# Attention with fp16-split operands: the row-maximum scores as two full-height matmuls instead of two half-height ones, and the maximum's rows moved behind the head's

## The chip, the cores and the metric

The kernel runs on one core of one Trainium2 chip. Its time is the device time of one execution in microseconds (us); the kernel before was timed three times. PE is TensorE (PEld its weight loads), DVE VectorE, ACT ScalarE, POOL GpSimd, SP the engine whose queue issues the DMAs. L532 is line 532 of the kernel before.

## What is computed

One pre-norm transformer block in float32 over x of 4 x 1024 x 128: layer norm, attention with 16 heads of 64, a residual, a second layer norm, and a gated feed-forward part (width 352) whose inputs and weights are quantised in blocks of 16. The attention, which holds nearly all of the work:

```python
q, k, v = (split_heads(ln(x) @ W.T) for W in (Wq, Wk, Wv))     # 4, 16, 1024, 64
sim  = einsum('bhid,bhjd->bhij', q, k) * 64 ** -0.5
e    = exp(sim - max(sim, axis=-1))
attn = e / (sum(e, axis=-1) + 1e-10)
x    = x + (attn @ v).reshape(4, 1024, 1024) @ Wo.T + bo
```

## The kernel before

**Work.** A pair of heads of one batch element is a round; there are 32, and `rounds` runs 34, since a round overlaps three pairs: the next pair's projections, this pair's scores and exponentials, and the previous pair's output (`flags` says which parts a round has). A round has four units `k` (head `k // 2`, half `k % 2` of its 1024 queries), and a unit eight slots `s`. Every engine has its own program in this order, written out by hand. The table `JOBS` says at which unit and slot PE, ACT and DVE do a round's other jobs (projections `k0` to `v1`, the transpose `m` of the maxima, `t`/`o` for the output projection, `x g u h d` for the feed-forward part); on PE all of them stand at odd slots. Those of the feed-forward part run in two-round cycles from round 9 on.

**Number format.** q and k are each split into a high and a low fp16 part. Per head there are four 1024-column operands: `q_hl` has q high in partitions 0 to 63 and q low in 64 to 127; `k_hh` has k high twice; `q_hm` and `k_l1` hold, in 64 partitions each, q high and k low, and beside them two rows with the (negative) row maxima and two rows of a constant, so that the product of the two adds k low times q high and subtracts each query's maximum. The other 62 partitions of the second pair are zeroed once (`ones`, L716 to L720).

**A slot on PE.** The transposed scores of 128 keys against 512 queries, in PSUM `st`: a matmul of 128 rows and 512 columns of `k_hh` and `q_hl` (L548), then one of `k_l1` and `q_hm` (L550). ACT takes the exponential (L658), POOL computes its fp16 low part (L415). Then eight matmuls of 129 columns for the unit before, which accumulate probabilities times v in `ob` (L576).

**The row maxima.** The maximum must be known before the exponentials, so two units ahead PE also computes the scores the other way round, 128 queries against 1024 keys, in the two PSUM banks of `sm`. This is `scores(s)` (L518 to L534), called at the start of each odd slot. It is two matmuls of 64 rows and 512 columns: the high part of q in partitions 0 to 63 of `q_hl` against keys 0 to 511, and the same numbers in partitions 64 to 127 of `q_hm` against keys 512 to 1023. The first waits until DVE's last reduction of `sm` is done (`s_mx`). DVE then reduces the 1024 columns to one maximum (L839) once both are done (`s_sm`). There are 16 such pairs of matmuls in a round, 512 in all, in rounds 0 to 31. After four, the job `m` transposes the maxima on PE (L505), ACT and DVE split them, and SP writes them into rows of `q_hm` (`place_max`, L315).

**What orders it.** DVE's program has its reduction of slot `s`, then the sums of `ob`, then the jobs of that slot and parts of the quantiser (L983 to L1009). It runs in that order whatever is ready.

Of the kernel before, what the change touches and what calls it, by code (L numbers as in the profile page):

```python
# [9 lines left out]
F16 = mybir.dt.float16  # L10
# [5 lines left out]
P = 128  # L16
B, N, DIM = 4, 1024, 128
# [117 lines left out]
def build(nc, x, wq, wk, wv, wo, bo, w_gate, w_up, w_down, out):  # L135
    with ExitStack() as ctx:
# [22 lines left out]


        q_hl = [sb(f"q_hl{n}", [P, N], F16) for n in range(4)]
        q_hm = [sb(f"q_hm{n}", [P, N], F16) for n in range(4)]
        k_hh = [sb(f"k_hh{n}", [P, N], F16) for n in range(4)]
        k_l1 = [sb(f"k_l1{n}", [P, N], F16) for n in range(4)]
        q_parts = [sb(f"q_{part}", [P, N], F16) for part in ("high", "low")]
        k_parts = [sb(f"k_{part}", [P, N], F16) for part in ("high", "low")]

# [47 lines left out]
        s_wh = sem("wT_high_made")  # L215
        s_we = sem("wT_low_made")
        s_init = sem("ones_made")
        s_qz = sem("max_rows_zeroed")
        s_kz = sem("ones_rows_zeroed")
        s_dl = sem("ln_step")  # L220
        s_rs = sem("rstd_step")
        s_xn = sem("xn_made")
# [72 lines left out]
        def _(sp):  # L295
# [9 lines left out]
            def round_(g, r, q):  # L305
                prev, cur, nxt = flags(r)

                def place_max(k):

                    head, half = (k + 1) // 2 % 2, (k + 1) % 2  # L310
                    n, u = 2 * (q if k < 3 else 1 - q) + head, (k + 1) % 2

                    wait(sp, s_mr, 4 * (g - 1) + k + 2)
                    for part, rows in enumerate((m_high, m_low)):
                        sp.dma_start(q_hm[n][part:part + 1, half * HALF:(half + 1) * HALF]  # L315
                                     .rearrange("a (t i) -> a t i", t=IT), rows[u][:, :]).then_inc(s_md[u], 16)

                if r == 0:
                    sp.wait_ge(s_qz, 4)
                if cur:  # L320
                    place_max(0)
                if nxt:
                    n = 2 * (1 - q)

                    wait(sp, s_hi, 4 * g + 2)
                    for h in range(2):
                        high = k_parts[0][h * DH:(h + 1) * DH, :]
                        sp.dma_start(k_hh[n + h][0:DH, :], high).then_inc(s_dk, 16)
                        sp.dma_start(k_hh[n + h][DH:P, :], high).then_inc(s_dk, 16)

                    wait(sp, s_lo, 4 * g + 2)
                    for h in range(2):
                        sp.dma_start(k_l1[n + h][DH:P, :], k_parts[1][h * DH:(h + 1) * DH, :]).then_inc(s_dk, 16)
                if cur:
                    place_max(1)
                if nxt:

                    wait(sp, s_hi, 4 * g + 4)
                    for h in range(2):
                        high = q_parts[0][h * DH:(h + 1) * DH, :]  # L340
                        sp.dma_start(q_hl[n + h][0:DH, :], high).then_inc(s_dq, 16)
                        sp.dma_start(q_hm[n + h][DH:P, :], high).then_inc(s_dq, 16)

                    wait(sp, s_lo, 4 * g + 4)
                    for h in range(2):
                        sp.dma_start(q_hl[n + h][DH:P, :], q_parts[1][h * DH:(h + 1) * DH, :]).then_inc(s_dq, 16)
                if cur:
                    place_max(2)
                if ffn_two(r, 2) is not None:
                    ffn.store(sp, out_t, s_out, x2, ffn_two(r, 2))  # L350
                if nxt:
                    place_max(3)
# [76 lines left out]
        def _(pe):  # L429
# [78 lines left out]
            def round_(g, r, q):  # L508
# [5 lines left out]
                for k in range(4):  # L514
# [3 lines left out]
                    def scores(s):  # L518

                        n = 2 * q + 1 if k < 2 else 2 * (1 - q)  # L520
                        if r == 0 and k == 2 and s == 1:

                            pe.wait_ge(s_we, 6)
                        if k == 2 and s == 1:
                            wait(pe, s_dk, 96 * (g + 1))
                            wait(pe, s_dq, 96 * (g + 1))

                        wait(pe, s_mx, 4 * (unit + 2) + s // 2)
                        t = half * IT + s // 2
                        for h, q_rows in enumerate((q_hl[n], q_hm[n])):  # L530
                            rows = slice(h * DH, (h + 1) * DH)
                            last = pe.matmul(sm[:, h, :], q_rows[rows, t * P:(t + 1) * P],  # L532
                                             k_hh[n][rows, h * 512:(h + 1) * 512], start=True, stop=True)
                        last.then_inc(s_sm, 2)  # L534

                    for s in range(SLOTS):
                        slot = 8 * k + s
# [15 lines left out]
                        if prev if k == 0 else cur:  # L553
# [24 lines left out]
                                                 skip_group_check=True)  # L578
                            if s % 4 == 3:
                                last.then_inc(s_pv, 1)  # L580
                        for n in jobs_at(ON_PE, r, k, s):
                            job(JOBS[n][0], g, r, q, n)
                if r == B - 2:
# [96 lines left out]
        def _(dve):  # L680
# [33 lines left out]
                                        ).then_inc(s_xe, 1)  # L714

            def ones(n):  # L716
                nc.vector.memset(q_hm[n][0:DH, :], 0.0).then_inc(s_qz, 1)
                nc.vector.memset(k_l1[n][0:DH, :], 0.0).then_inc(s_kz, 1)
                wait(dve, s_kz, n + 1)
                nc.vector.memset(k_l1[n][0:2, :], MAX_UNIT).then_inc(s_init, 1)  # L720

            nc.vector.memset(lift[:, :], SCALE * LIFT).then_inc(s_init, 1)
            nc.vector.memset(ones_8[:, :], 1.0).then_inc(s_init, 1)
# [628 lines left out]
```

## Time and profile before

| | |
|---|---|
| three runs | 1579.92, 1581.10, 1581.31 us; median 1581.1 |
| the profiled execution | 1579.92 us, its span 1578.1 us |
| busy share of the span | PE 93%, PEld 62%, DVE 76%, ACT 72%, POOL 79% |
| mean granted TensorE clock | 0.979 of full speed |
| chain that ended last, by engine | PE 76%, DVE 16%, POOL 4%, ACT 3% |
| chain, by line | ob L576 23%, st L548 14%, st L550 11%, sm L532 9%, DVE negm L839 5% |

Times are from the span's start. Matmuls are pipelined and their ends are modelled: a matmul of 512 columns is shown with 0.38 us, though the next one starts about 0.22 us after it. What PE costs is therefore read from start to start, not from the durations. An idle time in brackets names what ended it.

### The profile page before, as it was taken

To read this page: it belongs to the slowest core of one execution; us is meant where nothing else is said; L and a number is where in the kernel's file an instruction comes from. 1 tells how busy PE (TensorE), PEld (TensorE's weight loads), DVE (VectorE), ACT (ScalarE), POOL (GpSimd) and SP (SyncE) were. 2 spreads that over 40 slices of the span, in tenths; PEclk is the share of its full clock that TensorE was granted. 3 is DMA by queue.
4 is the path that set the end of the run, shared out by engine and by line. 5 is a ranking of instruction groups with operands and counts; after the bars stand their busy time and mean duration, and the time that the engine had idled before them with its cause. 6 is when DMAs were issued, how large, how long until landed. Compare 5 with 4: busy or idle time off the path is not lost.

```text
span 1578.1 us, 34995 instructions
## 1 busy us (share of the span) xinstructions
PE 1472.0 (93%) x13828; PEld 974.4 (62%) x13828; DVE 1191.8 (76%) x2057; ACT 1130.8 (72%) x2082; POOL 1244.6 (79%) x1345
## 2 busy tenths in 40 slices
PE   3799899999999999999999999999999999999965
PEld 2356666666666666666666666666666666666654
DVE  6777876666687868778786878878687887868667
ACT  2477777777877777777777777777777777777833
POOL 3488888888887878888787888878788887878842
PEclk9799999999999999999999999999999999999978
DMA  6100111111111111111111111111111111111000
GB/s 158 44 22 21 42 41 42 42 42 42 42 31 29 29 41 43 43 42 32 24 35 42 41 45 41 31 28 33 41 42 45 42 28 29 34 42 41 5 4 14
DMA packets 46658, 59.75 MB, mean 38 GB/s; under 512 B 8672, under 2 KB 21920, under 8 KB 46496
## 3 DMA queue, kind: packets, MB, share of 16 engines
q1 hardware_dynamic: 46496, 57.52, 15.5%
q8 instruction: 110, 1.80, 0.5%
q14 instruction: 52, 0.43, 0.1%
HBM read 4.80 MB, written 2.10 MB: 4 GB/s over the span
## 4 chain that ended last, share of the span: by engine, by line
PE 76%; DVE 16%; POOL 4%; ACT 3%; issue 1%; SPq 0%; DMA 0%; DVEq 0%; ACTq 0%; POOLq 0%
PE ob L576 23%; PE st L548 14%; PE st L550 11%; PE sm L532 9%; PE mb L476 5%; DVE negm L839 5%; PE mb L492 4%; POOL p_low L415 2%; PE mb L481 2%; PE mb L1108 2%; PE mb L487 2%; DVE xn L1082 2%; ACT probs L658 1%; DVE q_small L985 1%; PE mb L1119 1%
## 5 line engine op out<-in xcount | busy, mean ns | idle before, releaser
L415 POOL TENSOR_TENSOR p_low<-probs 128x512 f16<-128x512 f32 x1024 | 1092.1, 1078 | 249.8 <-ACT probs L658 245.8
L658 ACT ACTIVATE probs<-st,lift,exp_scale 128x512 f32<-128x512 f32 x1024 | 793.6, 775 | 251.0 <-PE st L550 228.6
L839 DVE TENSOR_REDUCE negm<-sm 128x1 f32<-128x1024 f32 x512 | 623.3, 1217 | 144.2 <-PE sm L532 141.1
L548 PE MATMUL st<-q_hl,k_hh 128*128 128x512 f16 x1024 | 394.4, 385 | 0.0
L550 PE MATMUL st<-q_hm,k_l 128*128 128x512 f16 x1024 | 389.0, 380 | 0.0
L576 PEld LDWEIGHTS ob<-v,p_low 128*128 128x128 f16 x4096 | 276.1, 97 | 124.0 <-POOL p_low L415 3.8
L576 PEld LDWEIGHTS ob<-v,probs 128*128 128x128 bf16 x4096 | 276.6, 98 | 121.0 <-issue 0.5
L576 PE MATMUL ob<-v,p_low 128*128 128x129 f16 x4096 | 317.6, 220 | 3.4 <-POOL p_low L415 3.4
L576 PE MATMUL ob<-v,probs 128*128 128x129 f16 x4096 | 318.0, 220 | 0.2
L532 PE MATMUL sm<-k_hh,q_hl 64*128 64x512 f16 x512 | 200.0, 391 | 53.1 <-DVE negm L839 43.9
L532 PE MATMUL sm<-k_hh,q_hm 64*128 64x512 f16 x512 | 200.1, 391 | 0.0
L548 PEld LDWEIGHTS st<-q_hl,k_hh 128*128 128x128 f16 x1024 | 99.1, 97 | 131.9 <-issue 109.1
L672 ACT ACTIVATE oscl<-ob,rden 128x128 f32<-128x128 f32 x512 | 158.4, 364 | 13.5 <-DVE rden L829 13.4
L422 POOL TENSOR_TENSOR o_n<-oscl 128x128 f32<-128x128 f32 x256 | 122.4, 478 | 6.6 <-ACT oscl L672 6.6
L532 PEld LDWEIGHTS sm<-k_hh,q_hl 64*128 64x128 f16 x512 | 47.4, 93 | 115.0 <-DVE negm L839 57.3
L550 PEld LDWEIGHTS st<-q_hm,k_l 128*128 128x128 f16 x1024 | 100.6, 98 | 16.3 <-issue 2.8
L820 DVE TENSOR_TENSOR x<-x,mb 128x512 f32<-128x512 f32 x64 | 44.0, 688 | 54.5 <-PE mb L492 54.5
L794 DVE SCALAR_TENSOR_TENSOR k_low<-mb,k_scale,k_high 128x512 f16<-128x512 f32 x64 | 47.8, 747 | 44.8 <-ACT k_high L622 44.8
L805 DVE TENSOR_TENSOR v<-mb,v 128x512 f16<-128x512 f32 x64 | 44.0, 688 | 49.6 <-ACT v L629 49.6
L629 ACT ACTIVATE v<-mb 128x512 f16<-128x512 f32 x64 | 38.2, 597 | 50.8 <-PE mb L481 49.2
L492 PE MATMUL mb<-wo_s,oT 128*128 128x128 f32 x512 | 69.7, 279 | 0.8 <-ACT oT L626 0.8
L492 PEld LDWEIGHTS mb<-wo_s,oT 128*128 128x128 f32 x512 | 63.1, 192 | 3.8 <-ACT oT L626 1.3
(164 smaller groups left out, 1528.1 us busy)
## 6 DMA issues: line engine op xcount, KB each, us to landing
k_hh<-k_high SPq DMA_DIRECT2D x128, 128.0 KB, 2.3
k_l<-k_low SPq DMA_DIRECT2D x64, 128.0 KB, 2.3
q_hl<-q_high SPq DMA_DIRECT2D x64, 128.0 KB, 2.3
q_hm<-q_high SPq DMA_DIRECT2D x64, 128.0 KB, 2.3
q_hl<-q_low SPq DMA_DIRECT2D x64, 128.0 KB, 2.3
x<-x SPq DMA_DIRECT2D x4, 512.0 KB, 7.2
q_hm<-m_high SPq DMA_DIRECT2D x128, 1.0 KB
q_hm<-m_low SPq DMA_DIRECT2D x128, 1.0 KB
```

What stands on the lines that cost most here:

```text
L415: return pool.tensor_tensor(p_low[b][:, j, :], p, p.bitcast(BF16)[:, 1::2], ALU.subtract)
L422: pool.tensor_tensor(o_n[pq][:, t:t + 2, head * DH:(head + 1) * DH], o[:, :, 0:DH], o[:, :, DH:2 * DH], ALU.add).then_inc(s_on, 1)
L476: last = pe.matmul(bank[:, :], of_pair(wT[w], "qk".index(name[0]), g), of_batch(xT[a], g, c * HALF, HALF), start=(w == 0 and a == 0), stop ...
L492: last = pe.matmul(bank[:, t * P:(t + 1) * P], oT[:, (4 * c + t) * P:(4 * c + t + 1) * P], wo_s[:, bass.ds((g - 2) % PAIRS, 1), :].rearran ...
L532: last = pe.matmul(sm[:, h, :], q_rows[rows, t * P:(t + 1) * P], k_hh[n][rows, h * 512:(h + 1) * 512], start=True, stop=True)
L548: pe.matmul(st[s % 2][:, :], k_hh[n][:, s * P:(s + 1) * P], q_hl[n][:, half * HALF:(half + 1) * HALF], start=True, stop=False)
L550: pe.matmul(st[s % 2][:, :], k_l1[n][:, s * P:(s + 1) * P], q_hm[n][:, half * HALF:(half + 1) * HALF], start=False, stop=True).then_inc(s_ ...
L576: last = pe.matmul(ob[bank][:, o:o + VC], p, v[pq][:, j, ph, 0:VC], start=(j == 0 and s % 4 == 0), stop=(j == JT - 1 and low == 1), skip_g ...
L658: nc.scalar.activation(probs[k % 2][:, s, :], st[s % 2][:, :], ACT.Exp, bias=lift[:, 0:1], scale=exp_scale[:, head, pair:pair + 1]).then_i ...
L672: last = nc.scalar.activation(oscl[bank][:, t, :], ob[bank][:, t * OT:t * OT + 2 * DH], ACT.Copy, scale=rden[:, bank, t:t + 1])
L794: nc.vector.scalar_tensor_tensor(out=k_parts[1][:, cols], in0=bank[:, :], scalar=k_scale[:, g % PAIRS:g % PAIRS + 1], in1=k_parts[0][:, cols],
L839: nc.vector.tensor_reduce(negm[k % 2][:, s // 2:s // 2 + 1], sm[:, :, :].rearrange("p a n -> p (a n)"), AX.X, ALU.max, negate=True).then_i ...
```

## The change

`scores` issues one matmul per slot instead of two per odd slot: `q_hl` against `k_hh`, both over all 128 partitions, so that the score for the maximum has k high times all of q, where it had k high times q high. The even slot's matmul (keys 0 to 511) is issued at the slot's end, before the jobs; the odd slot's (keys 512 to 1023) at its start, as before. Only the even one waits for DVE's last reduction; each counts 1 in `s_sm`. As `q_hm` is no longer read over its upper half here, it and `k_l1` shrink to 66 partitions: the head's 64 rows first, then the two rows of the maxima or of the constant. Their zeroing goes, with its two semaphores and SP's wait for it.

```diff
-        q_hm = [sb(f"q_hm{n}", [P, N], F16) for n in range(4)]
+        q_hm = [sb(f"q_hm{n}", [DH + 2, N], F16) for n in range(4)]
-        k_l1 = [sb(f"k_l1{n}", [P, N], F16) for n in range(4)]
+        k_l1 = [sb(f"k_l1{n}", [DH + 2, N], F16) for n in range(4)]
...
-                        sp.dma_start(q_hm[n][part:part + 1, half * HALF:(half + 1) * HALF]
+                        sp.dma_start(q_hm[n][DH + part:DH + part + 1, half * HALF:(half + 1) * HALF]
-                if r == 0:
-                    sp.wait_ge(s_qz, 4)
-                        sp.dma_start(k_l1[n + h][DH:P, :], k_parts[1][h * DH:(h + 1) * DH, :]).then_inc(s_dk, 16)
+                        sp.dma_start(k_l1[n + h][0:DH, :], k_parts[1][h * DH:(h + 1) * DH, :]).then_inc(s_dk, 16)
-                        sp.dma_start(q_hm[n + h][DH:P, :], high).then_inc(s_dq, 16)
+                        sp.dma_start(q_hm[n + h][0:DH, :], high).then_inc(s_dq, 16)
...
-                        if k == 2 and s == 1:
+                        if k == 2 and s == 0:
                             wait(pe, s_dk, 96 * (g + 1))
                             wait(pe, s_dq, 96 * (g + 1))
-                        wait(pe, s_mx, 4 * (unit + 2) + s // 2)
+                        if s % 2 == 0:
+                            wait(pe, s_mx, 4 * (unit + 2) + s // 2)
                         t = half * IT + s // 2
-                        for h, q_rows in enumerate((q_hl[n], q_hm[n])):
-                            rows = slice(h * DH, (h + 1) * DH)
-                            last = pe.matmul(sm[:, h, :], q_rows[rows, t * P:(t + 1) * P],
-                                             k_hh[n][rows, h * 512:(h + 1) * 512], start=True, stop=True)
-                        last.then_inc(s_sm, 2)
+                        pe.matmul(sm[:, s % 2, :], q_hl[n][:, t * P:(t + 1) * P],
+                                  k_hh[n][:, (s % 2) * 512:(s % 2 + 1) * 512], start=True, stop=True
+                                  ).then_inc(s_sm, 1)
...
                             if s % 4 == 3:
                                 last.then_inc(s_pv, 1)
+                        if has_max and not s % 2:
+                            scores(s)
                         for n in jobs_at(ON_PE, r, k, s):
...
             def ones(n):
-                nc.vector.memset(q_hm[n][0:DH, :], 0.0).then_inc(s_qz, 1)
-                nc.vector.memset(k_l1[n][0:DH, :], 0.0).then_inc(s_kz, 1)
-                wait(dve, s_kz, n + 1)
-                nc.vector.memset(k_l1[n][0:2, :], MAX_UNIT).then_inc(s_init, 1)
+                nc.vector.memset(k_l1[n][DH:DH + 2, :], MAX_UNIT).then_inc(s_init, 1)
```

What now stands in a row on PE in two slots of round 1, before (the number of columns stands last; `ob` is the group of eight):

```order
L576 MATMUL ob<-v,probs 128x129 x8
L532 MATMUL sm<-k_hh,q_hl 128x512
L532 MATMUL sm<-k_hh,q_hm 128x512
L548 MATMUL st<-q_hl,k_hh 128x512
L550 MATMUL st<-q_hm,k_l 128x512
L576 MATMUL ob<-v,probs 128x129 x8
L548 MATMUL st<-q_hl,k_hh 128x512
L550 MATMUL st<-q_hm,k_l 128x512
L576 MATMUL ob<-v,p_low 128x129 x8
```

and the same place of the changed kernel:

```order
L571 MATMUL ob<-v,probs 128x129 x8
L527 MATMUL sm<-k_hh,q_hl 128x512 x2
L543 MATMUL st<-q_hl,k_hh 128x512
L545 MATMUL st<-q_hm,k_l 128x512
L571 MATMUL ob<-v,probs 128x129 x8
L543 MATMUL st<-q_hl,k_hh 128x512
L545 MATMUL st<-q_hm,k_l 128x512
L571 MATMUL ob<-v,p_low 128x129 x8
```

The even slot's matmul is the last of its slot and the odd slot's the first of the next, and no job stands at an even slot: so the two are still neighbours, at the old place. What moved is only that both have the operand `q_hl`.

The start of DVE's program, before:

```order
L722 MEMSET lift 128x1
L723 MEMSET ones 8x128
L717 MEMSET q_hm 64x512
L718 MEMSET k_l 64x512
L720 MEMSET k_l 2x1024
...
L727 MEMSET v 128x16 x2
L688 BN_STATS stats<-x 128x6 x8
```

and now:

```order
L716 MEMSET lift 128x1
L717 MEMSET ones 8x128
L714 MEMSET k_l 2x1024 x3
L721 MEMSET v 128x16 x2
L685 BN_STATS stats<-x 128x6 x8
```

The three memsets L717 to L720 stood there three times, ahead of the first statistics of x; one of each three is left. A fourth set stands later in both.

## Rows read from the trace of the kernel before

**Rows 1.** Timeline, PE, steady slots (start us, us, engine, line, names, sizes, count).
```profile
669.30 0.62 PE L576 MATMUL ob<-v,probs 128*128 128x129 f16 x8
669.85 0.39 PE L532 MATMUL sm<-k_hh,q_hl 64*128 64x512 f16 x1
669.85 0.39 PE L532 MATMUL sm<-k_hh,q_hm 64*128 64x512 f16 x1
670.17 0.39 PE L548 MATMUL st<-q_hl,k_hh 128*128 128x512 f16 x1
670.40 0.38 PE L550 MATMUL st<-q_hm,k_l 128*128 128x512 f16 x1
...
672.05 0.39 PE L532 MATMUL sm<-k_hh,q_hl 64*128 64x512 f16 x1
```

**Rows 2.** Timeline, PE, three slots of round 32, without maxima and jobs.
```profile
1494.32 0.38 PE L548 MATMUL st<-q_hl,k_hh 128*128 128x512 f16 x1
...
1494.75 0.62 PE L576 MATMUL ob<-v,probs 128*128 128x129 f16 x8
...
1496.98 0.38 PE L548 MATMUL st<-q_hl,k_hh 128*128 128x512 f16 x1
```

**Rows 3.** Waits of PE to 62, to 480, to 1500 us (us, times, longest).
```profile
PE sm L532 <- DVE negm L839: 8.6, 7, 2.8
...
PE sm L532 <- DVE negm L839: 8.7, 8, 2.9
...
PE sm L532 <- DVE negm L839: 26.6, 44, 1.3
```

**Rows 4.** Timeline, PE, two waits of round 15.
```profile
687.21 0.39 PE L532 MATMUL sm<-k_hh,q_hl 64*128 64x512 f16 x1 [1.33 <-DVE negm L839]
...
719.01 0.39 PE L532 MATMUL sm<-k_hh,q_hl 64*128 64x512 f16 x1 [0.29 <-DVE negm L839]
```

**Rows 5.** Timeline, DVE, three reductions of round 15.
```profile
697.21 1.22 DVE L839 TENSOR_REDUCE negm<-sm 128x1 f32<-128x1024 f32 x1
...
717.74 1.21 DVE L839 TENSOR_REDUCE negm<-sm 128x1 f32<-128x1024 f32 x1
...
726.37 1.21 DVE L839 TENSOR_REDUCE negm<-sm 128x1 f32<-128x1024 f32 x1
```

**Rows 6.** Timeline, PE, the pairs behind the first and last of these.
```profile
698.51 0.39 PE L532 MATMUL sm<-k_hh,q_hl 64*128 64x512 f16 x1
...
727.79 0.39 PE L532 MATMUL sm<-k_hh,q_hl 64*128 64x512 f16 x1
```

**Rows 7.** Chain that ended last, in order of time, round 0 (start us, us, what).
```profile
40.69 0.63 PE sm L532 x2
```

**Rows 8.** Timeline, PE, at the start of round 1.
```profile
59.91 0.60 PE L532 MATMUL sm<-k_hh,q_hl 64*128 64x512 f16 x1 [0.35 <-DVE negm L839]
...
60.86 0.63 PE L550 MATMUL st<-q_hm,k_l 128*128 128x512 f16 x1
61.28 0.63 PE L476 MATMUL mb<-xT_high,wT_high 128*128 128x512 f16 x1
```

**Rows 9.** Busy time by stretch (us, busy us and count by engine, granted clock, DMA).
```profile
40.00:60.00 20.00, 10.73 (x53) 5.18 (x53) 14.43 (x21) 3.06 (x6) 2.34 (x1) 0.50 0.01 2
```

**Rows 10.** Timeline, DVE, from the start.
```profile
1.07 0.48 DVE L717 MEMSET q_hm<- 64x512 uint32 x1
...
2.37 0.91 DVE L720 MEMSET k_l<- 2x1024 f16 x1 [0.27 <-DVE k_l L718]
...
7.78 0.26 DVE L688 BATCH_NORM_STATS2 stats<-x 128x6 f32<-128x128 f32 x1
```

**Rows 11.** Tile x, to 12 us: its first DMA, and issue to landing.
```profile
L296 SPq DMA_DIRECT2D x<-x x1: 440/440/440, 0.7 to 0.7; - x1
...
DMA to landing us min/median/max: 4.2/7.2/7.4
```

**Rows 12.** Timeline, PE, matmuls of 128 and of 96 rows in turn.
```profile
720.23 1.55 PE L1119 MATMUL mb<-wdT,hiddenT 128*128 128x128 f32 x12
```

More of the change, by code:

```diff
@@ L217, in build @@
         s_init = sem("ones_made")
-        s_qz = sem("max_rows_zeroed")
-        s_kz = sem("ones_rows_zeroed")
         s_dl = sem("ln_step")
@@ L520, in scores @@
                         n = 2 * q + 1 if k < 2 else 2 * (1 - q)
-                        if r == 0 and k == 2 and s == 1:
+                        if r == 0 and k == 2 and s == 0:
                             pe.wait_ge(s_we, 6)
-                        if k == 2 and s == 1:
+                        if k == 2 and s == 0:
                             wait(pe, s_dk, 96 * (g + 1))
                             wait(pe, s_dq, 96 * (g + 1))
-                        wait(pe, s_mx, 4 * (unit + 2) + s // 2)
+                        if s % 2 == 0:
+                            wait(pe, s_mx, 4 * (unit + 2) + s // 2)
                         t = half * IT + s // 2
-                        for h, q_rows in enumerate((q_hl[n], q_hm[n])):
-                            rows = slice(h * DH, (h + 1) * DH)
-                            last = pe.matmul(sm[:, h, :], q_rows[rows, t * P:(t + 1) * P],
-                                             k_hh[n][rows, h * 512:(h + 1) * 512], start=True, stop=True)
-                        last.then_inc(s_sm, 2)
+                        pe.matmul(sm[:, s % 2, :], q_hl[n][:, t * P:(t + 1) * P],
+                                  k_hh[n][:, (s % 2) * 512:(s % 2 + 1) * 512], start=True, stop=True
+                                  ).then_inc(s_sm, 1)
                     for s in range(SLOTS):
```

## The prediction, made before the changed kernel was run

> **What bounds the kernel now.** I read the page's busy shares and the chain that ended last first: PE is busy 93% and carries 76% of the chain. Then PE's own waits. In the 1578 us it waits 59 times for DVE's reduction of the maxima, 43.9 us in all: 7 times before 62 us, 8 times up to 480 us, 44 times after [rows 3]. The 44 come in twos, four to each odd round from 11 to 31 (22 twos), where DVE works off the quantiser; even rounds have none. Everywhere else in rounds 1 to 31 PE's starts follow one another without a gap, so the kernel's time is PE's issue time, with DVE in its place at those spots, and a serial start-up of some 60 us.
>
> The price of a pair of maxima matmuls has to be read from start to start. The two half-height matmuls start together (669.85 both), and the next `st` matmul starts 0.32 us later, not 0.22. Ahead of them is a second gap: the group of eight `ob` matmuls starts at 669.30 and the pair 0.55 us later [rows 1], where a full-height `st` matmul follows such a group after (2.66 - 3 x 0.43) / 3 = 0.46 (three slots take 1496.98 - 1494.32 = 2.66 us, the two `st` matmuls of one 1494.75 - 1494.32 = 0.43) [rows 2]. From pair to pair, two slots take 2.20 us [rows 1]; two slots without a pair take 2/3 of 2.66, 1.77. The pair therefore costs 2.20 - 1.77 = 0.43 us of PE, although its matmuls run at once.
>
> **The change, part by part.**
>
> (a) *A pair where PE does not wait.* The new pair is two full-height matmuls of 512 columns, one after the other, in the same mode as their neighbours. Two of those take 0.43 us from start to start, as the two of `st` do [rows 2]. So the new pair costs 0.43 us as well: what is lost in parallel work is won in the gaps around it. With the rounding of the rows the difference is between -0.006 and +0.010 us a pair. I take +0.004, 2 x 0.2155 for the new against 0.427 for the old, a little above the middle. The difference applies to about 430 of the 512 pairs (59 wait; some 23 are tight, below): +1.7 us, bounds -2.6 and +4.3.
>
> The rule that speaks against the change is in the Trainium skill, page TensorE: Matmul & The Clock Gate, section Part 3: Packing small matmuls: matmuls in different row groups run concurrently, and the pack takes one matmul plus about 4 ns for each further one. By this alone the old pair costs 0.22 us, and the new one 0.22 more. The page TensorEngine Tiling (Array Packing), section Key Properties, adds that a change of tiling mode drains TensorE; the gaps of 0.09 before and 0.10 behind the pair in rows 1 agree with that, and the rows give 0.43.
>
> (b) *A pair for which PE waits.* The old one's gap in front lies inside the wait, so only the parallel work is lost. Before: pair to `st` 0.32, `st` to the second `st` 0.23 [rows 1], together 0.55. After: three full-height starts of 0.215 and the 0.01 that the first weight load shows behind a gap (0.23 against 0.22), 0.66. That is +0.11 a wait. Where two waits follow on each other, DVE is late through both and its clock sets the second, so the first's 0.11 only shortens the second wait (1.33 and 0.29 us long [rows 4], both above 0.11). 22 twos: +2.4 us. Of the 8 waits between 62 and 480 us six or seven count singly, one of them at the low clock: +0.8.
>
> (c) *Tight places.* Without the gap in front the new pair asks 0.09 us earlier. The reduction of 697.21 ends at 698.43, and PE's pair starts at 698.51 [rows 5, 6]. Where PE waits it starts 0.06 behind the reduction's end (717.74 + 1.21 = 718.95, then 719.01) [rows 4, 5]. So the new pair would come at 698.42 and start at 698.49: 0.02 earlier than the old one, then 0.11 more: +0.09. The second kind is at 727.79: the reduction of 726.37 ends at 727.58, but it hangs through a busy DVE on the pair before, whose second matmul now starts 0.45 + 0.215 instead of 0.55 us behind its `ob` group, 0.12 later. End 727.70, start 727.76, then 0.11 more: +0.08. There is one of the first kind in each of 11 rounds, one of the second in 12: 23 x 0.085 = +2.0. In the other pairs the reduction ends over 0.4 us ahead, which covers the 0.21 that goes, or about 0.2 ahead out of DVE's own backlog, which the pair's later end does not move, and there only 0.09 goes.
>
> (d) *Round 0, at the low clock.* From 40 to 60 us the granted clock is 0.50, the lower of its two levels, 1.2 GHz, with PE busy 10.7 of 20 us [rows 9]. A 512-column matmul takes 0.42 from start to start there [rows 8]. The chain passes six pairs there, the first at 40.69 [rows 7]. At two (40.69, 57.98) it goes on straight to DVE: the second matmul starts 0.43 later, +0.43 each. At four (42.62, 48.19, 53.67, 59.91) it goes on to PE's next work, which came after 0.54 (59.91 to 60.86 less the 0.41 of one `st` matmul [rows 8]) and now comes after 0.86: +0.32 each. Together +2.1 us. Nothing covers it; bounds 0 (if the chain finds another way) and +3.4 (all eight pairs of round 0 at 0.43).
>
> (e) *The memsets.* DVE begins with three sets of memsets at 1.07 us, each with 0.91 us that stay and two of 0.48 and a wait of 0.27 that go, and the first statistics of x start at 7.78 [rows 10]. The sets would end near 1.07 + 3 x 0.93 = 3.9, the two on v near 4.0. x is issued at 0.7 and lands 4.2 later, at 4.9 [rows 11]. So x becomes what is late: 4.95 instead of 7.78, -2.8 us. The whole start-up hangs on this one chain (statistics, root on POOL, norm, scales, transposes, projections, copies, 40.69); the weights that it meets on the way have landed by then. Bounds -2.8 and 0. The fourth set lies ahead of a wait of DVE for ACT and gives nothing.
>
> (f) *At nothing:* rows 64 and 65 instead of 0 and 1 in `q_hm` (the same number of DMAs and bytes, issued in the same order), SP's dropped wait (at 19 us, long before it has anything to send), and 66 rows instead of 128 in L550. A matmul costs its columns: the 12 that mix 128 and 96 rows take (1.55 - 0.27) / 11 = 0.116 us each, without a gap [rows 12]. If 66 rows did cost gaps as 64 do, see the fourth rival.
>
> Sum: 1.7 + 2.4 + 0.8 + 2.0 + 2.1 - 2.8 = +6.2 us. The profiled execution took 1579.9 us, so 1586.1. It is the fastest of the three; the median is 1.2 higher, so I forecast 1587.3 us, +0.4%.
>
> **The rivals.**
>
> 1. *The clock rises earlier in round 0 (not slower).* PE's new work between 40 and 60 us is about twice the old at these pairs, and the level could turn before 62 us, where it does now. At full clock the PE links of the chain from 43 to 63 us (some 7.2 us: twice the 12 matmuls of L481, twice four transposes, the first scores, a projection) take half, -3.6, and (d) falls from 2.1 to 0.7. The sum becomes +1.2: 1582.3. It decides if the granted clock is above 0.6 in that stretch. Against it: DVE's reductions, not PE, fill it, and PE stays idle half of the time.
>
> 2. *DVE hands the 0.12 us on.* Each reduction starts 0.12 later behind its pair. I let DVE's late stretches begin with something else (PE's other products, POOL's root), which holds as the rows between them show idle time of DVE ahead of them. If they begin with the reduction, each two of (b) costs 0.23 and not 0.11, and other places lose their slack: +2.6 and some 2 more: 1591.5.
>
> 3. *The old pair is dearer than I read it (faster).* If the second matmul on the same operand, or the missing gaps, save 0.01 us more a pair than the rows say, and PE's waits of (b) and (c) swallow their own losses, the memsets decide: 1581.1 - 2.8 - 4 + 2.1, about 1576.5. For it: (a) is a difference of two numbers of 0.43. Against it: the rows agree in several places to 0.005.
>
> 4. *The 66 rows bring the gaps of the half-height pair into every slot:* 1024 x about 0.2 = +200 us, 1790. And the packing rule at its word, 430 x 0.22 = +95, 1676. Rows 12 and rows 1 speak against the two.
>
> **How the numbers follow.** The forecast 0.60, its own range 1584.5 to 1590; rival 1 0.16, rival 2 0.12, rival 3 0.10, the two of rival 4 together 0.02. A measurement tells about 0.2% from no change, which is 1577.9 to 1584.3. Faster: most of rival 3, 0.08. Same: rival 1, the rest of 3, and the lower edge of the forecast, 0.24. Slower: 0.68. The range leaves out the end of rival 3 and of rival 2 and all of rival 4: 1581.0 to 1592.5.
>
> **What would show it.** In the changed profile the steady pair-to-pair time of two slots without jobs should be 2.20 to 2.21 us, with the `sm` matmuls 0.22 apart, `sm` 0.45 behind `ob`, and `st` 0.22 behind `sm`. Next to check are PE's waits for the reduction, as many as before plus about 23 short ones. In round 0 the pairs should be 0.43 apart, with the clock at 0.50, and the statistics should start near 4.95 and the first `sm` matmul near 37.9. The forecast is wrong if two slots take over 2.25 or under 2.18 us (a), if the start-up does not come forward, or if the waits in odd rounds grow in number beyond these.

## The result, and the profile after

The changed kernel takes 1599.5 us (median of four runs, 1598.2 to 1600.3), the kernel before 1580.5 (four runs, 1578.5 to 1581.3): ratio 1.0122, 95% interval 1.0109 to 1.0135. Forecast were 1587.3 us and a range of 1581.0 to 1592.5. It is slower, as forecast, but by three times as much. The profiled spans are 1578.1 and 1596.7 us, 18.6 apart. One run of all that follow, of x4_dve_late, took 1866 us at a mean granted clock of 0.75 where its five others have 0.98, and is left out.

The page of the changed kernel, its chain by engine and the groups that the change touches (count, busy us, mean ns of one, then the idle time ahead and its releaser):

```profile
PE 74%; DVE 19%; POOL 3%; ACT 3%; issue 1%; SPq 0%; DMA 0%; DVEq 0%; ACTq 0%; POOLq 0%
...
L833 DVE TENSOR_REDUCE negm<-sm 128x1 f32<-128x1024 f32 x512 | 624.2, 1219 | 155.1 <-PE sm L527 154.8
L545 PE MATMUL st<-q_hm,k_l 66*128 66x512 f16 x1024 | 390.8, 382 | 0.0
...
L527 PE MATMUL sm<-k_hh,q_hl 128*128 128x512 f16 x1024 | 308.6, 383 | 57.1 <-DVE negm L833 49.0
```

DVE's share of the chain rose from 16 to 19%. PE's waits for the reduction, in the same three stretches as [rows 3]:

```profile
PE sm L527 <- DVE negm L833: 7.4, 6, 2.5
...
PE sm L527 <- DVE negm L833: 10.6, 9, 2.9
...
PE sm L527 <- DVE negm L833: 31.0, 55, 1.2
```

They are 70 instead of 59 and 5.1 us longer in all. So part of the 18.6 us is new waiting, and the 12 new waits behind 62 us are one in each odd round from 9 to 31. PE's timeline in round 13, two slots without a projection or other long job and the new wait:

```profile
635.21 0.62 PE L571 MATMUL ob<-v,probs 128*128 128x129 f16 x8
635.67 0.59 PE L527 MATMUL sm<-k_hh,q_hl 128*128 128x512 f16 x2
636.10 0.38 PE L543 MATMUL st<-q_hl,k_hh 128*128 128x512 f16 x1
636.31 0.38 PE L545 MATMUL st<-q_hm,k_l 66*128 66x512 f16 x1
...
637.88 0.59 PE L527 MATMUL sm<-k_hh,q_hl 128*128 128x512 f16 x2
...
641.01 0.61 PE L527 MATMUL sm<-k_hh,q_hl 128*128 128x512 f16 x2 [0.65 <-DVE negm L833]
```

The pair stands 0.46 behind its `ob` group, `st` 0.43 behind the pair, and two slots take 2.21 us: what the forecast said of [rows 1], to 0.01. A hundredth counts 512 times, though. From the start of one pair to the same pair four rounds later (rounds 5 to 8, 64 pairs, no waits), before and after:

```profile
242.99 0.39 PE L532 MATMUL sm<-k_hh,q_hl 64*128 64x512 f16 x1
...
412.46 0.39 PE L532 MATMUL sm<-k_hh,q_hl 64*128 64x512 f16 x1
```

```profile
243.64 0.38 PE L527 MATMUL sm<-k_hh,q_hl 128*128 128x512 f16 x1
...
413.84 0.38 PE L527 MATMUL sm<-k_hh,q_hl 128*128 128x512 f16 x1
```

169.47 and 170.20 us: +0.73, or 0.0115 us a pair. The trace's starts in ns give a round of 42,367 and of 42,552 ns. They also show where it is: `ob` to `sm` 151 before and 60 after (behind the eighth `ob` matmul), `sm` to `st` 319 and 2 x 215, from that `st` to the second 227 and 215, and behind each 66-row matmul the next one starts after 220 ns instead of 216.

At the start of the program, DVE, for [rows 10]:

```profile
1.28 0.91 DVE L714 MEMSET k_l<- 2x1024 f16 x1 [0.27 <-issue]
...
4.97 0.68 DVE L685 BATCH_NORM_STATS2 stats<-x 128x6 f32<-128x128 f32 x3 [0.37 <-DMA x<-x]
```

and the stretch of [rows 9] with two parts of it (in each row from, to, length, then busy us of PE, PEld, DVE, ACT and POOL, the granted clock, DMA):

```profile
40.00:60.00 20.00, 13.69 (x55) 5.79 (x56) 14.64 (x22) 3.87 (x7) 3.38 (x2) 0.59 0.00 1
41.00:45.00 4.00, 2.58 (x15) 1.35 (x13) 3.21 (x8) 0.60 (x1) 0.00 (x0) 0.62 0.00 0
45.00:49.00 4.00, 2.88 (x20) 1.58 (x20) 3.18 (x4) 1.19 (x2) 2.34 (x1) 0.81 0.00 0
```

The k-th pair's start in both traces, subtracted, gives where the time went (pairs counted from 0, pair 8 is the first of round 1):

| up to | us | of it |
|---|---|---|
| the first pair (40.69, now 37.90) | -2.79 | the memsets |
| pair 12 (round 0, start of round 1) | +0.84 | pairs at the low clock |
| pair 72 (rounds 1 to 4) | +2.59 | 0.7 from 60 x 0.0115; 1.3 in one step at pair 45; 0.6 elsewhere |
| pair 136 (rounds 5 to 8) | +0.74 | 64 x 0.0115 |
| the last pair | +17.08 | 4.3 from 375 x 0.0115; 9.7 in twelve equal steps; 3.1 at the other waits and tight places of the two-round cycles |
| the end | +0.1 | |

A cycle of two rounds takes 92.18 us before and 93.61 after. Of these 1.44 us, 0.82 come at one pair, the one that waits at 641.01 (0.81 above the quiet price; it is the place of 727.79 in [rows 6], one cycle earlier). What DVE and POOL did ahead of it, before:

```profile
631.56 1.22 DVE L839 TENSOR_REDUCE negm<-sm 128x1 f32<-128x1024 f32 x1
631.66 1.04 POOL L415 TENSOR_TENSOR p_low<-probs 128x512 f16<-128x512 f32 x1 [1.93 <-ACT probs L658]
...
632.92 1.20 POOL L415 TENSOR_TENSOR p_low<-probs 128x512 f16<-128x512 f32 x1 [0.22 <-ACT probs L658]
632.95 0.27 DVE L998 TENSOR_SCALAR qw<-qv 128x256 uint32<-128x256 uint32 x1
633.26 1.01 DVE L1000 TENSOR_SCALAR qw<-qw 128x256 f32<-128x256 f32 x1
```

and after:

```profile
636.30 1.22 DVE L833 TENSOR_REDUCE negm<-sm 128x1 f32<-128x1024 f32 x1
636.32 1.04 POOL L411 TENSOR_TENSOR p_low<-probs 128x512 f16<-128x512 f32 x1 [1.97 <-ACT probs L655]
...
637.59 2.08 POOL L411 TENSOR_TENSOR p_low<-probs 128x512 f16<-128x512 f32 x2 [0.23 <-ACT probs L655]
...
637.70 1.07 DVE L992 TENSOR_SCALAR qw<-qv 128x256 uint32<-128x256 uint32 x1
638.81 1.01 DVE L994 TENSOR_SCALAR qw<-qw 128x256 f32<-128x256 f32 x1
...
639.75 1.21 DVE L833 TENSOR_REDUCE negm<-sm 128x1 f32<-128x1024 f32 x1
```

The same step of the quantiser, `qw<-qv`, takes 0.27 us in all twelve odd rounds before and 1.07 in all twelve after. It ends with POOL's product (637.70 + 1.07 = 638.77, the product 637.59 + 1.04 = 638.63). Before, it is POOL that pays: its product takes 1.20 where others take 1.04. The next step, `qw<-qw`, takes 1.01 in both kernels, though on 384 columns it takes 0.36 elsewhere. Before, it ends just behind the product that the first step had slipped past (632.92 + 1.20 = 634.12, the step 634.27); after, behind the next one. So the two steps wait for one product before and for two after, and the reduction behind them starts 1.86 us behind its pair instead of 0.89. The reduction ahead of them starts 1.09 behind its `ob` group where it had been 1.01 (0.08 later; 0.11 to 0.12 in quiet slots, where 0.12 was forecast). With it the step came 0.09 later against POOL's product (30 ns behind its start before, 116 after), and it lost to it.

The Trainium skill, page SBUF — State Buffer, section Who interferes with whom, has the rule: a VectorE instruction in a mode that uses both port pairs and a GpSimd instruction take the shared pair for their whole duration, and "Issue order, not op shape, decides who blocks." The traces agree at this place where the starts are 44 ns or more apart: the one that started second ends with or behind the other. Before, at 30 ns, it is POOL's product, the first by the records, that is longer, and x4_dve_late has another place where the starts in the trace do not tell who is held.

### The profile page after: what moved, and what is told of

Same layout as the page of the kernel before. It is cut to its first block, busy times and chain, and to the rows that moved or that the text cites. A ratio compares the mean times of both kernels' runs of the same rounds, so it can differ in the third digit from the quotient of the medians.

```text
span 1596.7 us, 34986 instructions
## 1 busy us (share of the span) xinstructions
PE 1488.5 (93%) x13828; PEld 1023.8 (64%) x13828; DVE 1208.6 (76%) x2049; ACT 1131.3 (71%) x2082; POOL 1240.7 (78%) x1345
## 4 chain that ended last, share of the span: by engine, by line
PE 74%; DVE 19%; POOL 3%; ACT 3%; issue 1%; SPq 0%; DMA 0%; DVEq 0%; ACTq 0%; POOLq 0%
PE ob L571 22%; PE sm L527 12%; PE st L545 11%; PE st L543 11%; DVE negm L833 6%; PE mb L472 5%; PE mb L488 4%; PE mb L477 2%; PE mb L1102 2%; PE mb L483 2%; POOL p_low L411 2%; DVE xn L1076 2%; ACT probs L655 1%; DVE q_small L979 1%; DVE v L799 1%; PE mb L1113 1%
## 5 line engine op out<-in xcount | busy, mean ns | idle before, releaser
L545 PE MATMUL st<-q_hm,k_l 66*128 66x512 f16 x1024 | 390.8, 382 | 0.0
L543 PE MATMUL st<-q_hl,k_hh 128*128 128x512 f16 x1024 | 388.6, 380 | 0.0
L527 PE MATMUL sm<-k_hh,q_hl 128*128 128x512 f16 x1024 | 308.6, 383 | 57.1 <-DVE negm L833 49.0
L545 PEld LDWEIGHTS st<-q_hm,k_l 66*128 66x128 f16 x1024 | 99.8, 97 | 76.8 <-issue 3.6
L527 PEld LDWEIGHTS sm<-k_hh,q_hl 128*128 128x128 f16 x1024 | 75.3, 97 | 77.0 <-DVE negm L833 65.9
L784 DVE TENSOR_TENSOR q_low<-mb,q_high 128x512 f16<-128x512 f32 x64 | 44.0, 687 | 28.9 <-ACT q_high L614 28.8
```

The costliest lines, as they stand in the source:

```text
L527: pe.matmul(sm[:, s % 2, :], q_hl[n][:, t * P:(t + 1) * P], k_hh[n][:, (s % 2) * 512:(s % 2 + 1) * 512], start=True, stop=True).then_inc(s ...
L543: pe.matmul(st[s % 2][:, :], k_hh[n][:, s * P:(s + 1) * P], q_hl[n][:, half * HALF:(half + 1) * HALF], start=True, stop=False)
L545: pe.matmul(st[s % 2][:, :], k_l1[n][:, s * P:(s + 1) * P], q_hm[n][:, half * HALF:(half + 1) * HALF], start=False, stop=True).then_inc(s_ ...
```

## The experiments

Theory A, for the quiet rounds: 8 of the 11.5 ns a pair are the two 66-row matmuls, the rest the new pair; its rival gives all to the new pair. Theory P, for the odd rounds: the loss is the collision with POOL, twelve times 0.8 us; its rival D: DVE is late by its own work, whatever POOL does. The expectations stand as written before each run. Each ratio is against runs of the kernel before beside it on the same chip, whose medians were 1579.7 to 1581.7 us.

**x1_rows128: the changed kernel with operands of 128 partitions.**

```diff
-        q_hm = [sb(f"q_hm{n}", [DH + 2, N], F16) for n in range(4)]
-        k_l1 = [sb(f"k_l1{n}", [DH + 2, N], F16) for n in range(4)]
+        q_hm = [sb(f"q_hm{n}", [P, N], F16) for n in range(4)]
+        k_l1 = [sb(f"k_l1{n}", [P, N], F16) for n in range(4)]
...
+                nc.vector.memset(q_hm[n][DH:P, :], 0.0).then_inc(s_qz, 1)
+                nc.vector.memset(k_l1[n][DH:P, :], 0.0).then_inc(s_kz, 1)
```

> The changed kernel with q_hm and k_l1 back at 128 partitions (head first, the two rows, 62 rows of zeros) and their zeroing back on DVE; the two full-height matmuls of the maxima stay. Theory A: of the 0.0115 us that each pair of slots lost, 0.008 comes from the two matmuls of 66 rows (the group of eight behind one starts 0.220 behind it, not 0.216) and 0.0035 from the new pair. Then the group is back at 0.216, a quiet round loses 16 x 0.0035 = 0.06 us against before (0.18 in the changed kernel), -4.1 us over 512 pairs, and the zeroing costs +2.8 again: about 1598, 1.3 us under the changed kernel. Rival B: the 0.008 belongs to the new full-height pair: the group stays at 0.220 and the time is the changed kernel's +2.8, 1602. In both the 256-column step of the quantiser (qw from qv) should still take 1.07 us.

Measured 1598.8 us, ratio 1.0108 (1.0095 to 1.0121). The quiet stretch:

```profile
247.02 0.38 PE L531 MATMUL sm<-k_hh,q_hl 128*128 128x512 f16 x1
...
416.68 0.38 PE L531 MATMUL sm<-k_hh,q_hl 128*128 128x512 f16 x1
```

It takes 169.66 us, 0.19 above before: 0.003 a pair is the price of two full-height matmuls against two half-height ones. The other 0.0085 was the 66 rows. (No other number of rows below 128 was run.) The start-up was back at 40.81, and `qw<-qv` stayed at 1.07 in all twelve. So theory A holds. The layout gave and took about the same (the 66 rows against the memsets), and nearly all of the loss is in the rest.

**x2_66rows: before, with only the 66 rows.**

```diff
-                            pe.matmul(st[s % 2][:, :], k_l1[n][:, s * P:(s + 1) * P],
-                                      q_hm[n][:, half * HALF:(half + 1) * HALF], start=False, stop=True
+                            pe.matmul(st[s % 2][:, :], k_l1[n][0:DH + 2, s * P:(s + 1) * P],
+                                      q_hm[n][0:DH + 2, half * HALF:(half + 1) * HALF], start=False, stop=True
```

> The kernel before, but its second matmul of st contracts over the first 66 partitions only (it leaves out 62 of the 64 products of k low and q high; the rows of the maxima are in). Theory A: the group of eight starts 0.220 behind it, 2 x 0.004 a pair of slots: +4.1 us, about 1584.6, if nothing else moves. Rival B: 66 rows cost nothing: 1580.5. A rival C, from the prediction, that they bring gaps like the half-height pair (about 0.2 us each): 1790; the changed kernel's profile already speaks against C.

Measured 1586.0 us, ratio 1.0030 (1.0018 to 1.0041). The quiet stretch:

```profile
247.18 0.39 PE L532 MATMUL sm<-k_hh,q_hl 64*128 64x512 f16 x1
...
417.16 0.39 PE L532 MATMUL sm<-k_hh,q_hl 64*128 64x512 f16 x1
```

169.98 against 169.47: 0.008 a pair, 4.1 us over 512, with `qw<-qv` at 0.27. Both edits give the same price for the 66 rows. (The whole is 4.7 us above before where 4.1 were expected; the profiled execution also lost some 3.6 us more in rounds 1 to 4, in ways told under x4_dve_late.)

**x8_same_rows: the half-height matmuls in the same half.**

```diff
-                        for h, q_rows in enumerate((q_hl[n], q_hm[n])):
-                            rows = slice(h * DH, (h + 1) * DH)
-                            last = pe.matmul(sm[:, h, :], q_rows[rows, t * P:(t + 1) * P],
+                        for h in range(2):
+                            rows = slice(0, DH)
+                            last = pe.matmul(sm[:, h, :], q_hl[n][rows, t * P:(t + 1) * P],
```

> The kernel before, with both half-height matmuls of a pair in partitions 0 to 63, so that they can't run at once; the result is the same. Reading of the prediction: the pair costs two gaps (0.09 and 0.10 us) around one matmul of 0.22 us; now 0.64 us instead of 0.43, two slots take 2.42 instead of 2.20, and the kernel takes about 450 x 0.215 = 97 us more, some 1680. Rival: the gaps belong to two row groups running at once, not to the change between 64 and 128 rows; then they go, and the pair costs 0.43: 1581 to 1585.

Measured 1675.9 us, ratio 1.0595 (1.0577 to 1.0613).

```profile
692.04 0.62 PE L576 MATMUL ob<-v,p_low 128*128 128x129 f16 x8
692.59 0.60 PE L532 MATMUL sm<-k_hh,q_hl 64*128 64x512 f16 x2
693.12 0.39 PE L548 MATMUL st<-q_hl,k_hh 128*128 128x512 f16 x1
```

The gaps of [rows 1] are still there: 0.55 behind `ob`, and 0.53 to `st` where it was 0.32. So the gaps come with the change between 64 and 128 rows, not with running side by side. The old pair saved 0.21 us by its overlap and lost 0.19 by the gaps, as (a) had read it.

**x4_dve_late: before, with 2 one-column memsets ahead of the step.** Nothing of PE's work is changed.

```diff
...
+                    if part == 2:
+                        for e in range(2):
+                            nc.vector.memset(self.spare2[:, e:e + 1], 0.0)
```

> The kernel before, with two one-column memsets on DVE ahead of the quantiser's step qw from qv of the 256-column input (12 times in all), which starts about 0.12 us later by it. Theory P: POOL and DVE shut each other out; in the kernel before this step starts in a gap of POOL (POOL's next low part starts at 632.92, the step at 632.95 and takes 0.27), and 0.1 us later it stands behind that instruction for its 1.04 us. Then it takes about 1.07 us, the pair of the next odd slot waits for its reduction, and the kernel is 12 x 0.8 = 9 us slower, about 1589, though it has the old pair of matmuls. Rival D: the changed kernel's loss there is a delay handed on by DVE, in proportion: 12 x 0.12 = 1.4 us, about 1582, and the step takes 0.27 us.

Measured 1587.4 us (median of the five runs kept), ratio 1.0038 (1.0025 to 1.0051); `qw<-qv` takes 1.14 in all twelve and a two-round cycle is 0.725 us longer.

```profile
637.09 1.04 POOL L415 TENSOR_TENSOR p_low<-probs 128x512 f16<-128x512 f32 x1 [0.22 <-ACT probs L658]
637.13 1.14 DVE L999 TENSOR_SCALAR qw<-qv 128x256 uint32<-128x256 uint32 x1
```

The step now starts 46 ns behind POOL's product in the records instead of 30, and that is enough: the trace has 12 x 0.725 = 8.7 us by it. (The records place the two memsets at 637.14, behind the step's start, though the program has them ahead of it. So 16 ns is a difference of records, and by how much the step really came later is not shown.) Theory D, which had 1.4 us and a step of 0.27, falls. The medians are 6.1 us apart (4 to 8 by the interval), less than 8.7; why is open.

This run shows something else. Up to 451 us its program is that of the kernel before, and yet its pairs fall 2.7 us behind in rounds 1 to 4: 1.2 at pair 45 and 1.6 at pair 52, where the granted clock was at the lower level from 189.3 to 192.7 us, behind a wait of PE of 1.69 us; the kernel before has that wait too, and its clock stayed at the upper level. At pair 45 stand a small step of the quantiser (DVE) and two products of POOL, before:

```profile
161.76 0.46 POOL L422 TENSOR_TENSOR o_n<-oscl 128x128 f32<-128x128 f32 x1
162.06 0.20 DVE L985 TENSOR_SCALAR q_small<-q_small 128x24 f32<-128x24 f32 x1
162.17 2.04 POOL L415 TENSOR_TENSOR p_low<-probs 128x512 f16<-128x512 f32 x2
```

and in x4_dve_late:

```profile
161.71 0.46 POOL L422 TENSOR_TENSOR o_n<-oscl 128x128 f32<-128x128 f32 x1
162.01 1.19 DVE L986 TENSOR_SCALAR q_small<-q_small 128x24 f32<-128x24 f32 x1
162.12 2.04 POOL L415 TENSOR_TENSOR p_low<-probs 128x512 f16<-128x512 f32 x2
```

Here the step starts 0.11 ahead of POOL's product, still beside the shorter one, and is held to the end of it all the same; before, 0.12 ahead, it passed. So the same program passes this place in one execution and loses there in another.

**x5_quant_first: the changed kernel, with the step ahead of the two sums of `ob`.**

```diff
+                        if (k, s) == (3, 1) and ffn_two(r, 0) is not None:
+                            at = ffn.steps(ffn_two(r, 0), False)
+                            ffn.quant(dve, ffn.small, ffn.xq[:, :], 2 * DIM, at, "first")
                         if s == 1 and (prev if k < 2 else cur):
                             sums(g, q, k, 1)
...
```

> The changed kernel, but on DVE the quantiser's step qw from qv of the 256-column input stands ahead of the sums of its slot, not behind them: it starts about 0.26 us earlier, near the end of the reduction, in the gap of POOL's low parts (637.36 to 637.59 in the changed kernel's profile). Theory P (the step waits behind the POOL instruction that started before it): it takes 0.27 us again, the pair behind does not wait 0.65, each odd round is 0.8 us shorter and the kernel 12 x 0.8 = 9.5 us faster than the changed one, about 1590. Rival D (the reductions' later start is handed on through a busy DVE): the order within the slot changes nothing, 1599, and the step still takes 1.07.

Measured 1588.8 us, ratio to before 1.0048 (1.0032 to 1.0063).

```profile
637.98 0.28 DVE L995 TENSOR_SCALAR qw<-qv 128x256 uint32<-128x256 uint32 x1
638.12 1.04 POOL L411 TENSOR_TENSOR p_low<-probs 128x512 f16<-128x512 f32 x1 [0.23 <-ACT probs L655]
```

The step starts 0.15 ahead of POOL's product and takes 0.28 in all twelve, and `qw<-qw` (0.87) ends behind this product and not the next. The cycle falls from 93.61 to 92.77, 12 x 0.85 = 10.2 us, and between the medians 10.7 of the 19 us lost are back, by an exchange in DVE's order alone. **x7_rows128_quant_first** is the same exchange on x1.

> x1_rows128 (two full-height matmuls, operands of 128 partitions, zeroing on DVE) with the order of x5_quant_first. Theory P: 12 x 0.8 under x1_rows128: 1598.8 - 9.5 = 1589, what is left against before being the waits (about 0.3 us an odd round), 0.003 us a pair, and one more such collision in round 3 (1.3 us). Rival D: 1598.8.

Measured 1588.8 us, ratio 1.0041 (1.0027 to 1.0056), 10.0 below x1, with `qw<-qv` at 0.28. Theory P holds from both sides.

**x3_pool_zero and x6_pool_zero_late: the start-up gain alone.** Before, with the zeroing on POOL (in x6 that of `q_hm` behind POOL's addition of the bias) and the sets of ones behind the first copies of x:

```diff
+            for n in range(4):
+                pool.memset(k_l1[n][0:DH, :], 0.0).then_inc(s_kz, 1)
...
+            for n in range(4):
+                pool.memset(q_hm[n][0:DH, :], 0.0).then_inc(s_qz, 1)
```

> The kernel before, with the zeroing of q_hm and k_l1 moved from DVE to POOL, and the three sets of ones moved behind the first copies of x (where the fourth stands). Both theories: the first statistics of x start near 4.95 us instead of 7.78, the first matmul of the maxima near 37.9 instead of 40.7, and the whole is 2.8 us faster, about 1577.7, if the start-up hangs on that chain. If only 1 us or less is won, the start-up was bound elsewhere, and the changed kernel's -2.8 us there came from something else.

> The kernel before, with the zeroing on POOL and the sets of ones moved as in x3_pool_zero, but POOL's zeroing of q_hm behind its addition of the bias. In x3 two tiny DVE steps of the head scales took 1.32 and 2.28 us while POOL had memsets and the bias. Theory P: with the bias done in time they take 0.16 each, the first matmul of the maxima comes near 37.9, and the kernel is 2.8 us faster than before, about 1578.4. Rival: the start-up stays at 40.7 or later (POOL's memsets still in the way, or another chain), 1581.

Measured 1581.4 us, ratio 1.0001 (0.9991 to 1.0011), and 1582.4, ratio 1.0004 (0.9995 to 1.0014). Both missed, x6 in the way that its own rival had it. The statistics came at 4.94 and 5.12, but the first pair only at 41.15 and 41.64. Timeline of DVE and POOL in x6:

```profile
22.59 0.28 DVE L755 TENSOR_REDUCE head_top<-mb 8x2 f32<-8x128 f32 x1 [1.23 <-PE mb L455]
22.67 3.62 POOL L395 MEMSET q_hm<- 64x1024 f16 x4
22.90 3.41 DVE L758 TENSOR_SCALAR head_top<-head_top 8x2 f32<-8x2 f32 x1
26.34 0.16 DVE L760 TENSOR_TENSOR head_diag<-ident,head_top 8x16 f32<-8x16 f32 x1
```

A DVE instruction on 8 x 2 numbers takes 3.41 us, up to the end of POOL's four memsets (22.67 + 3.62 = 26.29). The step ends with POOL's work here too, as at the other places, so it is taken for the same collision. In x3 three of the twelve places of `qw<-qv` were lost too (1.15 us).

**x10_memsets_late: the start-up gain without POOL.** Before, with DVE's memsets spread (and SP's wait for them further back):

```diff
-            for n in range(3):
-                ones(n)
+            ones(0)
...
-            ones(3)
+            ones(1)
...
+                        if r == 0 and (k, s) == (2, 0):
+                            ones(2)
+                            ones(3)
```

> The kernel before, with its row layout (both matmuls of a pair as before, one gap ahead and one behind) and its whole order, but with VectorE's four start-up memsets spread out: the first set of ones stays first, the second stands where the fourth stood, and the other two come in VectorE's idle time ahead of its first reduction. It asks for the start-up gain of the change alone, without its row layout and without a later reduction. Theory P (the loss of the change was the later start of VectorE's step at the odd rounds, plus the 66-row matmul and the pair): nothing of that is touched, so VectorE's step qw<-qv stays at 0.27 us in all 12 places, a quiet round stays at 42367 ns, the first statistics come near 4.95 us instead of 7.78, the first sm near 37.9 instead of 40.69, and the whole is 2.8 us shorter: about 1578. Rival S: the start-up gain is given back in rounds 1 to 4, where VectorE's and GpSimd's steps then meet at other phases (such shifts of 1 to 1.6 us stood in other kernels of this study); then the first sm is still near 37.9, but the offset is used up by the pairs of round 4: 1580 to 1581. Rival T: GpSimd or another engine's steps again hold VectorE's start-up, and the first sm does not come earlier: 1581.

Measured 1576.2 us, ratio 0.9984 (0.9976 to 0.9993). The first pair:

```profile
37.78 0.58 PE L532 MATMUL sm<-k_hh,q_hl 64*128 64x512 f16 x1 [7.79 <-DMA q_hl<-q_low]
```

The gain of (e) is real without the rest of the change: 2.9 at the first pair, 4.0 at the 72nd. At the end 3.3 are left, since one place of `qw<-qv` was lost (1.15). In 12 runs the kernel took 1574.6 to 1582.1 us.

**x11_both: x10 with the exchange of x5.** Its diff is the two together.

> The kernel with spread memsets (x10_memsets_late), and in the odd rounds VectorE's step qw<-qv ahead of the two sums of ob, as in x5_quant_first; the row layout is that of before. In x10 this step starts 30 ns behind GpSimd's product and is let through in 11 of 12 places (0.27 us, once 1.15). Theory P (what counts is which of the two starts first, and before and x10 stand a few ns from the edge): the step now starts some 0.2 us ahead of GpSimd's product, takes 0.28 in all 12 places and GpSimd's product 1.04 instead of 1.20 us; a two-round cycle is at most the 92174 ns of before; the time is that of x10 less its one collision of 0.72: 1575.5, and the runs lie within about 2 us of each other, where those of x10 went from 1574.6 to 1582.1. Rival Q: the sums of ob come 0.27 us later, ScalarE's scaling and what hangs on it follow, and the cycle grows: over 92300 ns, 1577 or more.

Measured 1576.4 us, ratio 0.9974 (0.9963 to 0.9985). In the trace all is as expected: `qw<-qv` 0.28 in all twelve, 0.23 ahead of POOL's product, the product 1.04, and the cycle 92.17 as before. The median is that of x10 within its scatter. The runs did not come to lie within 2 us of each other: 1574.4 to 1579.4 us, where the kernel before went from 1577.3 to 1584.7 on the same chip and from 1578.4 to 1581.1 on that of x10. So this place does not make the whole spread. Pair 45 and the granted clock, as told under x4_dve_late, differ between executions too; which of them makes the rest is open. x10 and x11 are the two that beat both kernels, by 0.16 and 0.26%.

## Why the prediction was right in direction and wrong in size

**The step that failed** is in (f) and (c): that beyond PE's own order everything keeps its duration, and that what comes 0.12 us later costs at most 0.12. The shift itself was about right (0.08 at this place, 0.11 to 0.12 elsewhere). But DVE's `qw<-qv`, which stood 30 ns behind POOL's product, came 116 ns behind it and was held for the product's length, and the step behind it for that of the next product. That is 12 x 0.81 = 9.7 us at the second kind of place of (c), for which 12 x 0.08 = 1.0 was set. x4 makes this loss with the old pair, x5 and x7 take it away with the new one. Rival 2 named the right cause, DVE handing the 0.12 on, but priced it at the shift itself. A second place of the kind makes the 1.28 at pair 45: there DVE's 128 x 24 step on `q_small` takes 1.03 instead of 0.20, behind a product of POOL that started 0.04 ahead of it. But x4, unchanged up to there, lost 1.2 at the same pair, so that these 1.3 us come from the change is not shown; it may be luck of the execution. The forecast looked at DVE's reductions and their slack and at no row of POOL beside DVE's other steps.

(a) was mis-sized. Per pair 0.0115, not 0.004. Of these, 0.003 is the new pair (x1), as predicted. The other 0.008 is the 66-row matmul, set at nothing by (f). Rows 12 compare matmuls of 128 columns, rounded to 0.01, which can't show 4 ns in 512 columns. From pair 12 on the quiet price comes to 5.8 us where 1.7 stood, and rival 4 asked only for gaps of 0.2.

(b) and (c), without the collision: 3.1 us in the twelve cycles against 3.4 forecast (22 twos at 0.11 and 11 tight places of the first kind at 0.09), near enough in sum. By the starts in ns a two costs 0.08 and a place of the first kind 0.03; small amounts at neighbouring pairs make up the rest. Of the 23 short new waits that should show, none is among the waits; the 12 new ones are those of the collision, 0.65 each. (Of the four waits of a cycle one lies in the last slot of the even round, so even rounds do have some.) The 0.8 for early waits stands beside 0.6 measured there.

(d) was +0.84 instead of +2.1. The clock showed 0.62 and 0.81 between 41 and 49 us, the upper level for part of it, where it had been 0.50 throughout; the later pairs of round 0 at 48.04 and 50.57 are at the low one again (1.03 us for the pair at 50.57 by the chain). That is rival 1 in part: the mean over 40 to 60 became 0.59, just under its mark of 0.6. Its reason, PE's new work, is not shown: in x10, which has the old pair, the upper level stood from 48.5 to 51.9 us, and the mean was 0.62.

(e) was right to the last digit that counts: statistics at 4.97 (4.95 forecast), first pair at 37.90 (37.9). With the zeroing back (x1) the pair was at 40.81, and x10 has the gain without the rest of the change.

By terms: -2.8 + 0.8 + 5.8 (a and the 66 rows) + 9.7 + 1.3 (the two collisions) + 3.1 + 0.6 (other early places) = 18.5, against a sum of 6.2. Of the 12.3 missing the collisions are 11.0 and the 66 rows some 4.2 (500 x 0.0085); (d), the waits and the small terms give the rest back.

## What to carry to other kernels

Before a step of DVE or POOL is moved, even by 0.1 us, look in the timeline for instructions of both engines that start within some tenths of each other, and for one line that shows two durations (0.27 and 1.07 here): at `qw<-qv` the one that started second paid the length of the other, times the number of repeats. Where the step was placed in POOL's idle time (in x11 0.02 ahead of that time), 0.15 to 0.23 us ahead of its product, it passed at all 36 places of x5, x7 and x11, and a mere exchange in DVE's order did it. A start 0.11 ahead while another instruction of POOL still ran was not enough (pair 45 in x4). Before two kernels are compared, look also at a stretch that is the same in both: what differs there is not the change. An edit that is set at nothing but stands in a loop of a thousand should be bounded in nanoseconds, from the difference of two starts many repeats apart.

## What the runs showed of the hardware

- At `qw<-qv` the edge between winning and losing is sharp. Over eight traces of twelve places each (before, after, x1 to x4, x6, x10): with POOL's product 22 to 32 ns ahead in the records, DVE's step was let through in all 51 places (0.27 us, and 0.16 fell on POOL); at 33 and 34 ns it was let through in five and held in four; at 44 to 122 ns it was held in all 36 (1.07 to 1.15). The kernel before stands at 29 to 33. These are differences of start times in the records: at pair 45 a step 0.11 ahead of the product was held in x4 and one 0.12 ahead passed in the kernel before.
- A matmul of 66 rows and 512 columns lets the next one start after 220 ns, one of 128 rows after 216 (medians of 1016 each, in the changed kernel and x2 against before and x1).
- A pair of 64-row matmuls between 128-row ones has gaps of 0.09 ahead and 0.10 behind; they are the same whether the two lie in different halves and overlap (before) or in the same half and follow one another (x8).
- In x6 a DVE instruction of 16 numbers took 3.41 us beside four memsets of POOL, which only write, and ended 0.02 us behind them; two rows on, one of 8 x 16 took 0.16.
- In round 0 the granted clock rose from the lower to the upper level for one stretch in the changed kernel (44.1 to 47.5 us; PE was busy 3.35 us from 40.1 to 44.1) and in x10 with the old pair (48.5 to 51.9 us; PE was busy 3.25 us from 44.5 to 48.5); before, it was 0.50 from 35.7 to 63.0 us. So such a rise is not proof of the change.
